# Where the second feed-forward's weights are quantised: from the second attention to the first, with two of the nine steps on GpSimd

## The reference

```python
# x: (16, 112, 256); ctx_1024: (16, 375, 256)
x = x + L0_xattn(layernorm(x), ctx_1024)      # 16 heads of 16
x = x + L0_ffn(layernorm(x))                  # 32 experts, top 6
x = x + L1_xattn(layernorm(x), ctx_1024)
x = x + L1_ffn(layernorm(x))

def fp4_quant_dequant(x):                     # blocks of 16 along the last dimension
    xb = x.reshape(shape[:-1] + (shape[-1] // 16, 16))
    scale = maximum(max(abs(xb), -1) / 6.0, 1e-12)
    xn = xb / scale
    idx = searchsorted(_MID, abs(xn))
    return (_GRID[idx] * sign(xn) * scale).reshape(shape)
def fp4_linear(x, w):
    return einsum('bsk,nk->bsn', fp4_quant_dequant(x), fp4_quant_dequant(w))
# L1_ffn: fp4_linear(silu(fp4_linear(x, w_gate)) * fp4_linear(x, w_up), w_down)
```

## Time and profile before

| | |
|---|---|
| median of 3 runs | 1109.3 us (1109.05 to 1110.9) |
| profiled execution, its time | 1109.39 us |
| profiled execution, span of its trace | 1107.6 us |
| TensorE busy | 944.3 us (85%) |
| VectorE busy | 696.9 us (63%) |
| ScalarE busy | 413.0 us (37%) |
| GpSimd busy | 136.5 us (12%) |
| mean granted TensorE clock | 0.958 |

### The profile page before, as it was taken

One profiled execution on the slowest core, in us unless ns is written; L12 is line 12 of the kernel. 1 busy time (PEld: TensorE's weight loads), 2 busy tenths in 40 slices (PEclk: granted clock), 3 DMA queues, 4 the chain that ended last, 5 costly groups with the idle time before them and its releaser, 6 DMA issues.

```text
span 1107.6 us, 24599 instructions
## 1 busy us (share of the span) xinstructions
PE 944.3 (85%) x7382; PEld 704.3 (64%) x7382; DVE 696.9 (63%) x1520; ACT 413.0 (37%) x966; POOL 136.5 (12%) x129
## 2 busy tenths in 40 slices
PE   3995999999988778989888866599999997798887
PEld 1663778788764365757766646377777775465555
DVE  4444677777548414343444455478888885799995
ACT  1341666666644430101101103256666665211111
POOL 7021000000012310000000000300000000344442
PEclk9997999999968999999999997799999999899999
DMA  9788444453115620201002121645354400000000
GB/s 272 195 231 178 91 94 84 85 104 78 58 42 139 190 72 24 62 24 47 28 24 76 38 82 42 136 82 100 85 99 88 90 16 3 0 12 12 12 12 17
DMA packets 129452, 86.58 MB, mean 78 GB/s; under 512 B 52195, under 2 KB 129123, under 8 KB 129379
## 3 DMA queue, kind: packets, MB, share of 16 engines
q1 hardware_dynamic: 129378, 85.58, 33.0%
HBM read 67.52 MB, written 17.79 MB: 77 GB/s over the span
## 4 chain that ended last, share of the span: by engine, by line
issue 36%; DVE 27%; PE 21%; DMA 6%; DVEq 4%; SPq 2%; POOL 2%; ACT 1%; POOLq 0%; ACTq 0%
PE ps L827 8%; DVE ext L1226 8%; PE ps L843 3%; DMA qscr<-qsp 2%; DVE Pr L1174 2%; DVE X L1375 2%; PE ps L589 2%; DMA Qz<-mT 2%; DVE Pr L1179 2%; DVE Pr L1177 2%; DVE amh L1406 1%; DVE Pr L1428 1%; PE ps L679 1%; POOL ksp L520 1%; PE ps L614 1%
## 5 line engine op out<-in xcount | busy, mean ns | idle before, releaser
L1226 DVE TENSOR_REDUCE ext<-ps 112x2 f32<-112x750 f32 x256 | 235.5, 933 | 57.7 <-PE ps L651 55.5
L999 ACT ACTIVATE Pr<-ps 125x448 f32<-125x448 f32 x384 | 199.1, 543 | 98.5 <-PE ps L665 85.0
L827 PE MATMUL ps<-xT,wgu 128*128 128x224 f32 x672 | 143.2, 364 | 16.6 <-issue 9.2
L827 PEld LDWEIGHTS ps<-xT,wgu 128*128 128x128 f32 x672 | 122.9, 191 | 38.8 <-issue 36.9
L665 PE MATMUL ps<-Qz,Kp 98*125 98x224 f16 x768 | 131.0, 266 | 16.2 <-DMA Qz<-mT 13.8
L651 PE MATMUL ps<-Kp,Qz 96*112 96x375 f16 x512 | 124.1, 334 | 13.4 <-DMA Qz<-qscr 12.2
L665 PEld LDWEIGHTS ps<-Qz,Kp 98*125 98x125 f16 x768 | 94.7, 137 | 49.9 <-DMA Qz<-mT 19.1
L719 PE MATMUL ps<-wv,ctx 128*125 128x256 f32 x384 | 121.2, 400 | 0.5 <-ACT Vx L1005 0.5
L589 PE MATMUL ps<-ctx,wk 128*128 128x375 f32 x256 | 95.9, 523 | 28.4 <-DMA bqk<-bqk 15.1
L1071 ACT ACTIVATE Pr<-ps 128x224 f32 x84 | 30.0, 357 | 227.3 <-PE ps L827 226.7
L1359 DVE TENSOR_TENSOR Pr<-Pr,ps (+1 forms) x84 | 32.6, 388 | 125.3 <-ACT Pr L1071 124.2
(11 more groups left out here) (140 smaller groups left out, 1088.3 us busy)
## 6 DMA issues: line engine op xcount, KB each, us to landing
ctx<-ctxT SPq DMA_DIRECT2D x64, 375.0 KB, 3.8
Kp<-kscr SPq DMA_DIRECT2D x96, 187.5 KB, 4.2
kscr<-ksp SPq DMA_DIRECT2D x32, 375.0 KB, 4.3
wgu<-wgu SPq DMA_DIRECT2D x32, 256.0 KB, 2.7
Qz<-qscr SPq DMA_DIRECT2D x192, 28.0 KB, 4.0
wdn<-wdn SPq DMA_DIRECT2D x32, 128.0 KB, 2.0
qscr<-qsp SPq DMA_DIRECT2D x32, 112.0 KB, 4.0
X<-x_in SPq DMA_DIRECT2D x1, 1792.0 KB, 12.5
```

The lines of the kernel that those rows point to most:

```text
L827: last = mm(ps[:, bass.ds((n & 1) + bank, 1), 0:CT], wgu_sb[par][:, q, EI * half_:EI * half_ + EI], xT2[:, q, c * CT:(c + 1) * CT], start= ...
L999: A(Pr[g % 2][0:KC, j, GI * t:GI * t + GI, :].rearrange("r h q -> r (h q)"), ps[0:KC, 4 + k % 2, 0:GI * S], ACT.Exp, scale=scale).then_inc ...
L1226: V.tensor_reduce(ext[0:S, 2 * p:2 * p + 2], ps[0:S, 2 * (p % 2):2 * (p % 2) + 2, 0:M], AX_X, red).then_inc(row_maximum_taken, 1)
```

## The change

All 16 pieces move from the second attention into the first, each to the batch of its number. The three steps that make scale and reciprocal and the four rounding steps stay on VectorE; the two products go to GpSimd, which does them with the same operands as before (`divide_weights`, `scale_weights`). The steps are staggered by a batch: in batch b VectorE makes the scales of piece b, then rounds piece b - 1, which GpSimd divided in the meantime. `scw`, and the scratch areas `qrw` and `qcw`, become two each. Seven places "q" stand in `DVE_ORDER`, and they do something in the first attention only. The last piece is rounded after the loop, ahead of the last `normalise`. ScalarE waits for all pieces before it touches the keys of the next stage (it fills `xT2` soon after).

The steps on VectorE are now joined by `Chain.link` (the three first rounding steps, the block maximum and the scale), so the wait stands on the instruction that follows, whichever it is.

```diff
-DVE_ORDER = "max max max max max max normalise max max split copy residual"
+DVE_ORDER = "max q max q max q max q max q max q normalise max q max split copy residual"
...
+            def divide_weights(b):
+                pool.wait_ge(weight_scales_ready, b + 1)
+                nc.gpsimd.tensor_tensor(blocks(qrw[b % 2]), blocks(fq[:, 16 * NW16 * b:16 * NW16 * (b + 1)]),
+                                        spread16(rcw), ALU.mult).then_inc(weights_divided, 1)
+
+            def scale_weights(b):
+                pool.wait_ge(weights_rounded, b + 1)
+                nc.gpsimd.tensor_tensor(blocks(fq[:, 16 * NW16 * b:16 * NW16 * (b + 1)]), blocks(qrw[b % 2]),
+                                        spread16(scw[b % 2]), ALU.mult).then_inc(weights_quantised, 1)
+
+            divide_weights(0)
+            for b in range(1, B):
+                divide_weights(b)
+                scale_weights(b - 1)
+            scale_weights(B - 1)
...
-            pe.wait_ge(weights_quantised, 9 * B)
+            pe.wait_ge(weights_quantised, B)
...
                 if l == 0:
+                    act.wait_ge(weights_quantised, B)
...
-                wait_from(dve, weights_quantised, b * 9 + k)
                 if k == 0:
-                    last = V.tensor_reduce(amw[:, :], blk(w0), AX_X, ALU.max, apply_absolute_value=True)
+                    ch.link(V.tensor_reduce(amw[:, :], w0.rearrange("p (b e) -> p b e", e=16), AX_X, ALU.max,
+                                            apply_absolute_value=True))
...
+                    if b >= 2:
+                        dve.wait_ge(weights_quantised, b - 1)
+                    ch.link(V.tensor_scalar(scw[b % 2][:, :], amw[:, :], 1.0 / 6.0, 1e-12, ALU.mult, ALU.max))
                 else:
-                    last = V.tensor_tensor(blk(w0), blk(qrw), spread(scw), ALU.mult)
-                last.then_inc(weights_quantised, 1)
+                    if b >= 1:
+                        dve.wait_ge(weights_divided, b)
+                    V.reciprocal(rcw[:, :], scw[b % 2][:, :]).then_inc(weight_scales_ready, 1)
+
+            def round_weights(b, k):
+
+                if k == 0:
+                    dve.wait_ge(weights_divided, b + 1)
+                last = fp4_step(128, qrw[b % 2], qcw[b % 2], 16 * NW16, k)
+                if k < 3:
+                    ch.link(last)
+                else:
+                    last.then_inc(weights_rounded, 1)
...
-                if l == 1:
+                if l == 0:
                     dve.wait_ge(ffn_weights_loaded, 16 * 5)
                     dve.wait_ge(padding_set, 7)
...
+                        elif step == "q" and l == 0:
+                            k = next(steps)
+                            if k < 3:
+                                quantise_weights(b, k)
+                            elif b > 0:
+                                round_weights(b - 1, k - 3)
+                if l == 0:
+                    for k in range(4):
+                        round_weights(B - 1, k)
                 normalise(g0 + B - 1)
```

More of the change, by code:

```diff
@@ L159, in build @@
         fq = sb("fq", [128, 3 * 6 * D])
-        amw, scw, rcw = (sb(n, [128, NW16]) for n in ("amw", "scw", "rcw"))
+        amw, rcw = (sb(n, [128, NW16]) for n in ("amw", "rcw"))
+        scw = [sb(f"scw{p}", [128, NW16]) for p in (0, 1)]
         NX, NH = D // 16, FI // 16
@@ L184, in build @@
         fdT = spare[:, 2 * C2 * FI:2 * C2 * FI + 6 * D].rearrange("p (c o) -> p c o", c=6)
-        qrw, qcw = (xT2[:, n, 0:16 * NW16] for n in (0, 1))
+        qrw, qcw = ([xT2[:, n, 16 * NW16 * p:16 * NW16 * (p + 1)] for p in (0, 1)] for n in (0, 1))
         ps = ctx.enter_context(nc.psum_tensor("ps", [128, 8, 512], F32))
@@ L257, in build @@
         ffn_weights_loaded = sem("ffn_weights_loaded")
+        weight_scales_ready = sem("weight_scales_ready")
+        weights_divided = sem("weights_divided")
+        weights_rounded = sem("weights_rounded")
         weights_quantised = sem("weights_quantised")
@@ L515, in _ @@
             add_bias(0)
+            pool.wait_ge(ffn_weights_loaded, 16 * 5)
+            spread16 = lambda t: t[:, :].rearrange("p (b o) -> p b o", o=1).broadcast_to([128, NW16, 16])
+            blocks = lambda t: t.rearrange("p (b e) -> p b e", e=16)
+            def divide_weights(b):
[11 more added lines that the diff above has]
+            scale_weights(B - 1)
             with pool.Fori(0, B // 2) as i:
@@ L1151, in quantise_weights @@
             def quantise_weights(b, k):
-                n, w0 = 16 * NW16, fq[:, bass.ds(b * (16 * NW16), 16 * NW16)]
-                blk = lambda t: t.rearrange("p (b e) -> p b e", e=16)
-                spread = lambda t: t[:, :].rearrange("p (b o) -> p b o", o=1).broadcast_to([128, NW16, 16])
-                wait_from(dve, weights_quantised, b * 9 + k)
+                n, w0 = 16 * NW16, fq[:, 16 * NW16 * b:16 * NW16 * (b + 1)]
                 if k == 0:
-                    last = V.tensor_reduce(amw[:, :], blk(w0), AX_X, ALU.max, apply_absolute_value=True)
+                    ch.link(V.tensor_reduce(amw[:, :], w0.rearrange("p (b e) -> p b e", e=16), AX_X, ALU.max,
+                                            apply_absolute_value=True))
                 elif k == 1:
[L1160 to L1166, removed]
-                else:
-                    last = V.tensor_tensor(blk(w0), blk(qrw), spread(scw), ALU.mult)
-                last.then_inc(weights_quantised, 1)
+                    if b >= 2:
+                        dve.wait_ge(weights_quantised, b - 1)
+                    ch.link(V.tensor_scalar(scw[b % 2][:, :], amw[:, :], 1.0 / 6.0, 1e-12, ALU.mult, ALU.max))
+                else:
+                    if b >= 1:
[9 more added lines that the diff above has]
+                    last.then_inc(weights_rounded, 1)
             def fp4_step(p, r, c, n, k):
@@ L1266, in _ @@
                 for b in range(B):
-                    g, pairs, pieces = g0 + b, iter(range(PAIRS)), iter(range(9))
+                    g, pairs, steps = g0 + b, iter(range(PAIRS)), iter(range(7))
                     for step in DVE_ORDER.split():
```

## The result

The changed kernel takes 1114.1 us (median of 20 runs) against 1109.98 us for the kernel before (median of 20 runs, taken beside them). The ratio is 1.0032, with a 95% interval of 1.0017 to 1.0047: slower by 3.6 us, 1.9 to 5.2. The forecast was +3.8. The profiled execution took 1117.07 us (span 1115.2), 3 us more than the median.

The account below looks back on a forecast made before the run. TensorE was taken to bound the first attention, VectorE's run from first maximum to split the second. +14.7 (first) - 10.9 (second) = +3.8 us on 1109.4, the median 0.1 below: 1113.1 us, range 1108.3 to 1118.5.

Parts of the forecast that it names:

- The bound: Kernel before: TensorE bounds the first attention; VectorE's unbroken run from first maximum to split costs the second 0.75 us a batch.
- Second attention, -10.9: Second attention, nine steps leave: 0.75 us gained in each of 14 batches and about 0.4 in the one before.
- (a): First attention's VectorE run: one step fewer, as the product by the reciprocal goes to GpSimd; minus 0.36 us a batch.
- (c): First attention's VectorE run: the eighth maximum has no step behind it and the split waits for its end; plus 0.13 us.
- the run: First attention, from TensorE's first R to M: 10.48 - 0.36 + 0.61 + 0.13 = 10.86 us, against TensorE's own 9.74.
- (b): First attention's VectorE run: five new semaphore waits a batch from `Chain.link`, 0.12 to 0.13 us each; plus 0.61 us.
- (d): First attention: GpSimd's products, some 0.81 us, beside VectorE's rounding steps; the first rounding step ends 0.02 us later: nothing.
- rival 3: First attention: a GpSimd product of 1.1 us holds up VectorE's first rounding step; +4.2, 1117.3 us; chance 0.16.
- How many batches: First attention: 14 batches pay 1.12 us, less 1.0 us had back in three with transfer waits; 14.7 us.
- The tail: After the loop: the last piece's four rounding steps, about 1.54 us, fit VectorE's idle 1.65 before the last `normalise`; no cost.
- Rival 1: First attention: the five waits are free, the run is 10.25 us; -4.1, whole 1105.2 us; chance 0.10.
- Rival 2: First attention: VectorE's idle time, 2.9 us a batch, takes all 2.4 added; only -10.9 stays, 1098.4 us; chance 0.05.
- Rival 4: Cost to the first attention about equals the second's gain (waits of 0.07 to 0.09, or more transfer stalls); within 2 us of 1109.3; chance 0.09.

Follow-up runs that it names:

- e2: Kernel before with the nine quantisation steps moved to the first attention, all on VectorE, none on GpSimd; 1114.07 us, ratio 1.0027 to the kernel before.
- e1: Changed kernel with quantisation steps joined by their own semaphore, the wait on the next such step, not the row maximum between; 1108.69 us, ratio 0.9977.
- e3: Changed kernel with GpSimd's product by the reciprocal done twice, the first time into unused memory; 1111.72 us in one execution.
- e5: e3 with one wait more: the first rounding step also waits for the row maximum just ahead of it; 1120.77 us in one execution.
- e4: e1 with only three steps left among the maxima, four placed later, and GpSimd's products in the other order; 1100.63 us, ratio 0.9921.

## Why the prediction was right, point by point

**The bound.** Right. The first attention was at TensorE's pace, the second at VectorE's run from the first maximum to the split. e2 shows that the loss of 0.75 us follows the steps.

**Second attention, -10.9.** First M to last M was 199.8 and 200.1 us in two executions of before, and 191.1, 188.6 and 187.2 in three of the change: a mean of 189.0, 11.0 less. The profiled execution alone would have given 8.8, and a reader of that profile would call the term wrong. But three executions that spread over 3.9 us don't show a term to 0.1. Four more traces have the changed kernel's second attention, instruction for instruction (e1, e2, e3, e5: 191.0, 189.6, 189.3, 190.4); all seven give 189.6, or 10.4 less. The 0.75 a batch is sure (12.97 to 12.22), the exact sum isn't.

**(a) to (c), the run.** Forecast 10.86 us from R to M, measured 10.89; forecast period 13.34, measured 13.37. (b) was five waits at 0.12, and e1 has them at 0.13 each. (a) and (c) together were 0.23, and e1 against e2 has 0.24. Of the waits forecast for TensorE (some 0.7 at T, some 0.4 at M) the rows show 0.39 and 0.25 in brackets. Read as delays the forecast holds: T stands 0.78 later behind the first R than before, and M another 0.37. The brackets are shorter since they count from the recorded end of the instruction ahead, which T's start had preceded by 0.17 before, and since the last R already comes 0.17 late.

**(d), GpSimd.** The value, nothing, was right, the reason only in part. I took the product for 0.81 us from the rows of 256 and 704 columns; alone it takes 0.68. (The row of 256 columns, 0.77 us, was no product alone either: it began beside a running step of VectorE, 955.87 to 956.33, and the shortest of its kind in that stage takes 0.62.) And I took VectorE's step to be the one that stands. In the batches that count it was GpSimd that stood, for 0.78 us, with 11.6 us left until the first instruction that waits for its end (the next batch's reciprocal). Neither way round would have cost anything here: with GpSimd first, the forecast's own working gives the step's end at 179.98 + 0.68 + 0.14 = 180.80, and it ended at 180.90. It is with a longer product that the order matters: e5 is 0.57 us a batch above e3, its own wait included. Had the product been longer, as in e3, I would have been wrong by 0.5 us a batch: the point of 0.79 us from which I let rival 3 decide was not one. The Trainium skill, "SBUF — State Buffer", section "Who interferes with whom", says that whoever issues first has the port and the other blocks. That one of the two blocks the other is seen in both directions (0.73 for a step of 0.30 in e5, 1.46 for a product of 0.68 in the change). Which one issues first isn't to be read from the starts in the trace: GpSimd's comes first in both. No run here shows the moment of issue.

**How many batches.** 14 x 1.12 - 1.0 = 14.7 was forecast. The 14 distances are 188.2, 188.4 and 188.0 against 173.1 and 173.9, 14.7 on the mean. The transfer stalls, 0.86 and 0.94 us before, were 0.46 and 0.55 in the change: 0.4 hidden in each, where 0.34 was forecast; the third, 0.12 before, is gone. (In the second execution of the kernel before they were 1.57, 1.37 and 0.03, so the 1.0 in all is one execution's number.)

**The tail.** VectorE's last `normalise` wasn't delayed: TensorE waited 0.81 us for its result before and after alike.

**The rivals.** Rival 1 (waits are free, 1105.2) is what e1 gives to the change: a batch of 12.73. The rule behind it, which the Trainium skill, "VectorE: DVE Perf Modes", section "The DRAIN you can't avoid", takes from eight copies in a row, doesn't hold for this kernel's steps: 0.36 without the wait, 0.48 with it. Rival 2 (idle time takes it all) fell as stated, 1.15 us lost with VectorE idle in 2.3 of 13.37. But its number, 10.9 us less, lies within e4's interval (6.0 to 11.4), where the steps went to the idle time. Rival 3 didn't come, for the reason above. Rival 4 (waits of 0.07 to 0.09, the whole within 2 us of 1109.3) fell with the waits at 0.13.

**The number.** Forecast +3.8 us, measured +3.6 with an interval of 1.9 to 5.2. The run and its price are shown to a few hundredths of a microsecond; that the whole agrees to 0.2 is partly luck.

## What to carry to other kernels

An engine's idle share says nothing about what can be added to it; look for the stretch between the instruction that starts its run and the one that others wait for, and put work outside of it. A semaphore wait between two steps of one engine belongs on the second step, not on whatever is interleaved between them: here the wait on a stranger costs 0.13 us each time, five times a batch. Moving work to another engine or stage gave 0.24 us a batch and nothing; placing six of the nine steps behind the point that the others wait for gave all 0.75.

## What the runs showed of the hardware that I had not expected

A GpSimd product of 128 x 288 takes 0.68 us alone and 1.46 when a TENSOR_SCALAR of VectorE without an open wait stands queued behind a running row maximum; it then ends 0.53 to 0.54 us behind that step's end, at three places (the change, and both products of e3). VectorE loses nothing there. With a semaphore wait on the TENSOR_SCALAR it is the other way round: 0.68 and 0.73 (e5), and 0.68 and 0.72 in the last batch of the change. A TENSOR_SCALAR queued without an open wait behind an addition of 0.36 us stands too (1.42 us at 1077.32 of the kernel before), so being queued isn't the whole condition. GpSimd's record starts before the step's in all these cases, so the starts in the trace don't tell who will stand. The row maxima, which read PSUM, and the product by the scale beside them didn't hinder each other (0.93 to 0.94 and 0.68 us).
